# Probabilities split without GpSimd, three output tiles multiplied after the FFN loop, and DMAs issued inside attention, in a cross-attention and ternary FFN kernel

## The reference

```
x = x + xattn(layernorm(x), ctx)          # x (4, 2048, 512), ctx (4, 154, 512)
x = x + ffn(layernorm(x))
xattn: q = x @ Wq.T -> q1, q2 of 16 heads x 32;  k1, k2, v from ctx, 8 kv heads
       w = softmax(q1 k1') - lam * softmax(q2 k2');  a = w @ v
       a * rsqrt(mean(a^2) + eps) * g * (1 - lam_init) @ Wo.T
ffn:   h = gelu(layernorm(x; g1, b1) @ ternary(w1).T + bias1)      # 512 -> 2048
       layernorm(h; g2, b2) @ ternary(w2).T + bias2                # 2048 -> 512
```

## Time and profile before

| what | value |
|---|---|
| median of three runs | 2513.64 us |
| the profiled execution | 2510.21 us, span 2508.4 us |
| PE busy | 2191.9 us, 87% of the span |
| DVE, ACT, POOL busy | 76%, 58%, 54% |
| mean granted TensorE clock | 0.923 of 2.4 GHz |
| chain that ended last | PE 42%, DVE 17%, issue 9%, SPq 9%, ACT 7% |

### The profile page before, as it was taken

How to read it: one execution, slowest core, us unless ns; L and a number is a source line. 1 busy time by engine, 2 the same in 40 slices (tenths; PEclk the granted TensorE clock), 3 DMA queues, 4 the chain that set the end, 5 groups by cost and what they waited for, 6 DMA issues and landing times.

```text
span 2508.4 us, 45318 instructions
## 1 busy us (share of the span) xinstructions
PE 2191.9 (87%) x18239; PEld 1217.8 (49%) x18239; DVE 1913.5 (76%) x3030; ACT 1456.4 (58%) x1973; POOL 1344.7 (54%) x931
## 2 busy tenths in 40 slices
PE   7777979889797988989798898979889898998968
PEld 5344445445454544445454444545445454554543
DVE  4776779778687877868787786878768787877763
ACT  3574656656465665556566554656646466664544
POOL 2333737546383754638365473846537384663627
PEclk9868989999898999989899998989989898998979
DMA  8313122131312213121321313122141211312010
GB/s 292 99 45 83 28 74 63 40 81 52 85 33 73 64 40 81 50 70 36 86 65 40 81 45 73 38 70 67 40 95 40 72 44 56 81 40 64 23 30 17
DMA packets 253009, 160.16 MB, mean 64 GB/s; under 512 B 171812, under 2 KB 221580, under 8 KB 252288
## 3 DMA queue, kind: packets, MB, share of 16 engines
q1 hardware_dynamic: 249792, 152.07, 23.0%
q0 software_dynamic: 3008, 5.20, 0.7%
HBM read 51.82 MB, written 20.38 MB: 29 GB/s over the span
## 4 chain that ended last, share of the span: by engine, by line
PE 42%; DVE 17%; issue 9%; SPq 9%; ACT 7%; DMA 1%; POOL 1%; DVEq 0%; POOLq 0%; ACTq 0%
PE ps L1581 17%; PE ps L1603 9%; SPq L517 8%; PE ps L1487 5%; DVE arena L1261 3%; ACT arena L812 2%; DVE attn_raw L1146 2%; DVE attn_raw L1151 2%; PE ps L1515 2%; DVE p L1133 1%; DVE attn_raw L1155 1%; PE ps L1593 1%; ACT p L815 1%; DVE attn_raw L1160 1%; ACT arena L810 1%
## 5 line engine op out<-in xcount | busy, mean ns | idle before, releaser
L686 POOL TENSOR_TENSOR attn_raw<-attn_raw 128x512 f32<-128x512 f32 x448 | 642.4, 1453 | 51.6 <-ACT attn_raw L841 23.2
L1581 PE MATMUL ps<-rows,w1T 128*128 128x512 f16 x2048 | 491.2, 383 | 31.2 <-DVE rows L1221 31.2
L1109 DVE TENSOR_REDUCE arena<-ps 128x3 f32<-128x462 f32 (+1 forms) x704 | 403.7, 613 | 43.3 <-PE ps L1487 41.5
L1226 DVE SCALAR_TENSOR_TENSOR arena<-attn_raw,vec_cols,arena 128x512 f16<-128x512 f32 x256 | 278.6, 1088 | 62.0 <-ACT arena L839 58.5
L836 ACT ACTIVATE attn_raw<-ps,vec_cols,wstep 128x512 f32<-128x512 f32 x256 | 198.5, 775 | 183.4 <-PE ps L1581 181.4
L1581 PEld LDWEIGHTS ps<-rows,w1T 128*128 128x128 f16 x2048 | 191.9, 98 | 230.3 <-DVE rows L1221 43.5
L810 ACT ACTIVATE arena<-ps 128x1024 f32<-128x1024 f32 x128 | 130.8, 1022 | 297.5 <-PE ps L1515 297.5
L657 POOL TENSOR_TENSOR q<-q 128x512 f16<-128x512 f32 x128 | 201.8, 1578 | 169.8 <-ACT q L801 168.5
L1603 PE MATMUL ps<-w2T,arena 128*128 128x512 f16 x1088 | 271.1, 378 | 0.0
L799 ACT ACTIVATE q<-ps 128x512 f32<-128x512 f32 x128 | 77.0, 602 | 329.8 <-PE ps L1437 189.9
L664 POOL TENSOR_TENSOR p<-arena,p 128x1024 f16<-128x1024 f32 x64 | 137.8, 2153 | 242.5 <-ACT p L815 242.5
(11 more groups left out here) (195 smaller groups left out, 5073.4 us busy)
## 6 DMA issues: line engine op xcount, KB each, us to landing
stack_raw<-q SPq DMA_DIRECT2D x744, 64.0 KB, 2.0
arena<-in_x SPq DMA_DIRECT2D x64, 256.0 KB, 2.7
out<-arena SPq DMA_DIRECT2D x64, 256.0 KB, 2.0
arena<-in_x SPq DMA_DIRECT2D x14, 1024.0 KB, 5.9
arena<-in_L_ffn_w SPq DMA_DIRECT2D x7, 1024.0 KB, 14.4
rows<-in_x SPq DMA_DIRECT2D x2, 1024.0 KB, 6.9
stack_raw<-in_L_xattn_Wq SPq DMA_DIRECT2D x8, 256.0 KB, 9.2
k_att<-k_store SPq DMA_DIRECT2D x4, 495.0 KB
```

The lines of the kernel that those rows point to most:

```text
L686: ins = pool.tensor_tensor(acc[:, e, :], acc[:, e, :], src[:, j % NG, :], ALU.add)
L1109: dve.tensor_reduce(negmax[:, tt, u0:u1], ps[:, row_bank(c, tb), 0:(u1 - u0) * S].rearrange("p (u s) -> p u s", s=S), AX.X, ALU.max, negat ...
L1226: dve.scalar_tensor_tensor(gg16[:, j, 1, :], gelu_t[:, j % NG, :], g2_col[:, j:j + 1], gg16[:, j, 0, :], ALU.mult, ALU.subtract).then_inc( ...
L1581: ins = pe.matmul(ps[:, B_H + j % 2, :], w1T[:, k, j * P:(j + 1) * P], rows16[:, e, k, :], start=(k == 0 and e == 0), stop=(k == KD - 1 an ...
```

## The change

The splitting of probabilities leaves POOL: ACT casts slices 0, 1 and then 2 to 4, DVE computes lo of both parts. In the FFN loop only row tile 0 is multiplied; tiles 1, 2 and 3 are "late". The first group's upper scores go to banks 5 to 7, so that group no longer waits for the gelu sums and two output tiles; the second group does. The stores, the reloads of x, the transposes of the attention output and the first pair of query stacks are issued by SP in the order of `ATTEND`.

```diff
-    "e2 g f2 y0 y1 y2 s0 q0 z0 z1 z2 s1 h3 v0 s2 i3 v1 y3 z3 s3 q1 v2 s4 q2 t0 v3 s5 q3 v4 s6 t1 v5 s7 v6 t2 v7").split()]
+    "e1 c g e2 s0 e3 y0 y1 q0 s1 h1 v0 z0 z1 s2 h2 v1 y2 s3 q1 t0 z2 v2 s4 h3 v3 s5 h4 t1 y3 v4 s6 q2 z3 v5 s7 t2 q3 v6 v7").split()]
+LATE1 = 0
+LATE = {("e", 1): (1, LATE1, 10), ("e", 2): (1, 10, 14), ("e", 3): (1, 14, JH),
+        ("h", 1): (2, 0, 8), ("h", 2): (2, 8, JH), ("h", 3): (3, 0, 8), ("h", 4): (3, 8, JH)}
-            return 2 + tt if tt < 2 else B_Q
+            return (2, 3, B_Q, B_Q)[tt]
+        def upper_banks(c, gi):
+            return slice(2, 5) if gi or c == 0 else slice(5, 8)
...
             def iteration(i):                                # SP
-                if i:
-                    store(i - 1, 0)
-                    for tt in range(1, TT):
-                        store(i - 1, tt)
-                        load_x_res(i, tt - 1)
-                    load_x_res(i, TT - 1)
+                for what, n in ATTEND if i else ():
+                    if what == "z":
+                        store(i - 1, n)
+                        if n:
+                            load_x_res(i, n - 1)
+                    elif what == "t":
+                        transpose_attn(i, n)
+                        if n == 0 and i + 1 < NBLK:
+                            stack_queries(i + 1, 0, i)
...
-                    for p in range(0 if i else QATT // 2, QM // 2):
+                    for p in range(1 if i else QATT // 2, QM // 2):
                         stack_queries(i + 1, p, i)
...
-            def probs_lo(c, gi):                             # POOL
-                wait(pool, s_p_hi, c, 2 * QM, 2 * gi + 1)
-                split = p_split[gi % 2]
-                pool.tensor_tensor(split[:, 1, 0:2, :], probs[:, gi % 2, 0:2, :], split[:, 0, 0:2, :],
-                                   ALU.subtract).then_inc(s_lo_pool, 1)
...
-                for half in range(2):                        # ACT
+                for half, slices in enumerate((slice(0, 2), slice(2, 5))):
                     wait(act, s_p, c, 2 * QM, 2 * gi + half + 1)
-                    act.copy(split[:, 0, 2 * half:2 * half + 2, :],
-                             probs[:, buf, 2 * half:2 * half + 2, :]).then_inc(s_p_hi, 1)
+                    act.copy(split[:, 0, slices, :], probs[:, buf, slices, :]).then_inc(s_p_hi, 1)
...
-                dve.tensor_copy(split[:, 0, 4, :], probs[:, buf, 4, :]).then_inc(s_r_hi, 1)
-                wait(dve, s_p_hi, c, 2 * QM, 2 * gi + 2)
-                wait(dve, s_r_hi, c, QM, gi + 1)
-                dve.tensor_tensor(split[:, 1, 2:5, :], probs[:, buf, 2:5, :], split[:, 0, 2:5, :],
-                                  ALU.subtract).then_inc(s_lo_dve, 1)
+                for half, slices in enumerate((slice(0, 2), slice(2, 5))):
+                    wait(dve, s_p_hi, c, 2 * QM, 2 * gi + half + 1)
+                    ins = dve.tensor_tensor(split[:, 1, slices, :], probs[:, buf, slices, :], split[:, 0, slices, :],
+                                            ALU.subtract)
+                ins.then_inc(s_p_lo, 1)
...
+                elif n == 0 and c >= 2:                      # PE, queries
+                    wait(pe, s_p, c - 1, 2 * QM, 2)
                 elif n == 1:
                     if c >= 2:
-                        wait(pe, s_y, c - 2, TT, TT)
+                        wait(pe, s_y, c - 2, TT, 3)
...
+                    if n == 2 and c >= 2:
+                        wait(pe, s_y, c - 2, TT, TT)
...
                     if c:                                    # PE, scores of group 0
-                        wait(pe, s_gln, c - 1, 1, 1)
-                        wait(pe, s_y, c - 1, TT, 2)
+                        wait(pe, s_gelu, c - 1, JH, JH)
...
+                elif gi == 1 and c:
+                    wait(pe, s_p, c, 2 * QM, 1)
+                    wait(pe, s_gln, c - 1, 1, 1)
+                    wait(pe, s_y, c - 1, TT, 2)
...
                     if j == 0 and tt == 2:                   # PE, ffn_late
-                        wait(pe, s_gelu, c, JH, JH)
-                    elif j == 0:
+                        wait(pe, s_p, c + 1, 2 * QM, 2)
+                    elif j == 0 and tt == 3:
                         wait(pe, s_y, c, TT, tt)
+                        if c + 2 < NBLK:
+                            wait(pe, s_q32, c + 2, QM, 2)
+                    elif tt == 1:
+                        wait(pe, s_gg_lo, c, JH, j + 1)
...
-                banks = (2, 3) if ahead else range(TT)
+                banks = (2,) if ahead else range(TT)
```

More of the change, by code:

```diff
@@ L327, in build @@
             "row_scores", "row_max", "negmax_hi", "negmax_lo", "negmax_transposed", "negmax_copied", "negmax_stacked"))
-        s_s, s_p, s_p_hi, s_r_hi, s_lo_dve, s_lo_pool, s_pv, s_inv, s_norm, s_att = (sem(n) for n in (
-            "scores", "probs", "probs_hi", "rest_probs_hi", "probs_lo_by_dve", "probs_lo_by_pool", "values_done", "inverse_sum",
+        s_s, s_p, s_p_hi, s_p_lo, s_pv, s_inv, s_norm, s_att = (sem(n) for n in (
+            "scores", "probs", "probs_hi", "probs_lo", "values_done", "inverse_sum",
             "values_normed", "attn_ready"))
@@ L490, in load_x_in @@
                 if c >= 2:
-                    wait(sp, s_lo_dve, c - 2, QM, QM - 1)
-                    wait(sp, s_lo_pool, c - 2, QM, QM - 1)
+                    wait(sp, s_p_lo, c - 2, QM, QM - 1)
                 sp.dma_start(x_in if c >= 2 else x_in0, x_blk[c]).then_inc(s_xin, 16)
@@ L559, in iteration @@
                     transpose_ternary(JH + 12)
-                elif i + 1 < NBLK:
-                    for p in range(QATT // 2):
-                        transpose_attn(i, p)
                 if i + 1 < NBLK and (i + 1) % BLK_PER_BATCH == 0:
                     load_keys((i + 1) // BLK_PER_BATCH)
-                if i + 1 < NBLK:
+                if i:
+                    load_x_res(i, TT - 1)
+                else:
                     transpose_attn(i, KD - 2)
@@ L581, in iteration @@
                     stack_maxima(i + 1)
-                else:
-                    for mp in range(KD):
-                        transpose_attn(i, mp)
             setup()
@@ L696, in iteration @@
                         power(3, s_gln, s_rstd4, i - 1)
-                    elif what == "s":
-                        probs_lo(i, n)
                     elif what == "q" and ahead:
@@ L811, in exponentials @@
                 wait(act, s_s, c, 2 * QM, 2 * gi + 2)
-                act.activation(probs[:, buf, 2:5, :], ps[:, 2:5, :], ACT.Exp).then_inc(s_p, 1)
-                for half in range(2):
+                act.activation(probs[:, buf, 2:5, :], ps[:, upper_banks(c, gi), :], ACT.Exp).then_inc(s_p, 1)
+                for half, slices in enumerate((slice(0, 2), slice(2, 5))):
                     wait(act, s_p, c, 2 * QM, 2 * gi + half + 1)
-                    act.copy(split[:, 0, 2 * half:2 * half + 2, :],
-                             probs[:, buf, 2 * half:2 * half + 2, :]).then_inc(s_p_hi, 1)
+                    act.copy(split[:, 0, slices, :], probs[:, buf, slices, :]).then_inc(s_p_hi, 1)
             def attn_hi(c, mp):
@@ L1506, in scores @@
                     if c:
-                        wait(pe, s_gln, c - 1, 1, 1)
-                        wait(pe, s_y, c - 1, TT, 2)
+                        wait(pe, s_gelu, c - 1, JH, JH)
                     if 0 < c < NBLK - 1:
                         wait_rows(pe, s_xt_lo, s_xd, c + 1)
+                elif gi == 1 and c:
+                    wait(pe, s_p, c, 2 * QM, 1)
+                    wait(pe, s_gln, c - 1, 1, 1)
+                    wait(pe, s_y, c - 1, TT, 2)
                 else:
                     wait(pe, s_p, c, 2 * QM, 2 * gi)
+                upper = upper_banks(c, gi).start
                 for i in range(UPT):
                     u = UPT * gi + i
-                    ins = pe.matmul(ps[:, i, :], k_att[0:STKM, key_unit(u), 0:P], stack[0:STKM, u, :], start=True, stop=True)
+                    ins = pe.matmul(ps[:, i if i < 2 else upper + i - 2, :], k_att[0:STKM, key_unit(u), 0:P], stack[0:STKM, u, :], start=True, stop=True)
                     if i == 1:
@@ L1526, in values @@
                 mp, split = ORDER[gi] % (QM // 2), p_split[gi % 2]
-                wait(pe, s_lo_dve, c, QM, gi + 1)
-                wait(pe, s_lo_pool, c, QM, gi + 1)
+                wait(pe, s_p_lo, c, QM, gi + 1)
                 wait(pe, s_norm, c, QM, gi)
@@ L1629, in iteration @@
                         values(i, n)
-                    elif what == "e" and i:
-                        ffn_late(i - 1, n, range(JH // 4))
+                    elif (what, n) in LATE and i:
+                        tt, j0, j1 = LATE[what, n]
+                        ffn_late(i - 1, tt, range(j0, j1))
+                    elif what == "c" and i:
                         transpose_maxima(i)
-                    elif what == "f" and i:
-                        ffn_late(i - 1, n, range(JH // 4, JH))
```

(4 more changed lines are left out.)

6 lines of the change are left out of this document (2 added, 4 removed).

## The result

The kernel after takes **2531.78 us** (2530.05 to 2533.56), the kernel before, on the same chip, 2513.15: ratio 1.0073, 95% interval 1.006 to 1.0085, or 18.6 us slower. The forecast was 2511, with faster the likeliest side: the time lies inside the range and on the wrong side. The profiled execution has a span of 2528.2 us against 2508.4.

What follows compares the result with a forecast made beforehand. The FFN loop was held by PE, DVE and POOL together. A block's -1.3 + 4.1 - 2.6 = +0.2 gave +3 us over 14 blocks, block 0 -5, last block 0: 2511 us, range 2465 to 2550.

Steps and rivals of the forecast that it cites:

- Part 1: FFN loop: PE sheds 6.9 us but DVE doesn't follow; maxima transposed 53.15 us after loop start, against 51.83 before.
- e1, 20 matmuls, 4.3 us: Loop's end: row tile 1's 20 late matmuls behind DVE's last gelu lo, before the maxima's transposes, take 4.3 us.
- Part 2: Loop's end to first scores: scores wait for DMAs of the maxima, starting at 58.2 against 59.52, -1.3 us a block.
- Part 3: Attention: new gaps, POOL's lo of query 3 and 3.0 us of half clock give 65.2 against 61.14, +4.1 us.
- its load stays: Attention: DVE loses a cast, gains a lo of about 1.2 us, no longer meets POOL, so its load is unchanged.
- Part 4: Attention to FFN loop: early query stacks free query 6, removing 2.6 of PE's 2.63 us wait, -2.6 us a block.
- Block 0: First block's loop: PE busy 65.80 of 67.00 us, so the 6.9 us saved count, less new waits: -5 us.
- The last block: Final block of the kernel: no change, 0 us.
- Half clock and POOL stay out of attention: Faster rival: attention takes 60.8 to 62.2 us; 2469 us, or another 20 less; chance 0.26.
- The loop does shorten: Faster rival, FFN loop: gelu's lo falls towards 0.73 us, DVE ends up to 3 us earlier; 2470 us; chance 0.11.
- The opening goes to half clock: Slower rival: idle time around first scores puts 4 to 5 us at half clock; attention 68, 2550 us; chance 0.18.
- Query 6 not freed: Slower rival, before the FFN loop: SP reaches pair 1 late, the 2.6 us stay; 2548 us; chance 0.05.

Runs made afterwards that it cites:

- sp_only: Kernel before with SP's order alone changed (stores, tile reloads, attention transposes, first pair of query stacks issued inside attention): 2473.62 us, ratio 0.9851 to before.
- tiles_first: Kernel after with row tile 1 finished before the first scores and output tiles 0 and 1 added ahead of group 0's lo: 2494.98 us, ratio 0.9927 to before.
- after_tile2_first: Kernel after with one token moved, DVE adding output tile 2 ahead of group 1's normalise step: 2487.07 us, ratio 0.9886 to before.
- after_old_split: Kernel after with the old splitting of probabilities (POOL's subtractions, ACT's two casts, DVE's cast as before): 2611.13 us, ratio 1.0386 to before.
- dense_loop: Kernel after with row tile 1 multiplied twice, once more in the FFN loop, 32 unused matmuls a block: 2545.82 us, ratio 1.0128 to before.

## Why the prediction was wrong, point by point

- **Part 1, the end of the loop: right in kind, wrong in size.** That DVE doesn't follow held: in blocks 1 to 14 a lo in the loop takes 1.20 us in the mean, against 1.11 before, POOL's 28 sums still have no break, and PE idles. The last lo ends 48.94 us after the loop's start (1181.52 + 1.81 - 1134.39) where I said 48.3; beside POOL's sums it took 1.81, where it had taken 1.01. The step that failed is the next one: "e1, 20 matmuls, 4.3 us". I took full clock straight behind the idle time that I had just derived. It was 6.0, so the maxima were transposed at 55.44 and not at 53.15.
- **Part 2: its increments right, its base wrong.** From the transposes to the scores 4.85 us (forecast 4.92), released by the DMA of the maxima. Loop and tail were 60.3 us in nine of the ten blocks where the clock fell (58.2 in block 14, whose loop is shorter), and 58.6 in the four where it didn't; I said 58.2. The ten slow tails cost 10 x 1.7 = 17 us, nearly the whole 18.6 by which the kernel is slower: without them it would be within measurement of the old one. (This is the account against the forecast. By parts the same 18.6 is about -78 - 26 + 121.)
- **Part 3: total right, one claim wrong.** Attention 65.2 forecast, 64.99 measured, and the walk can be checked gap by gap: 0.95, 3.0, 2.5, 0.6 and about 4 forecast; 0.82, 2.67, 2.47, 0.50 and 4.35 in block 6. Half clock was taken at 3.0; PE is busy 54.79 us where its work at full clock is 50.6, so 4.2. POOL's lo of query 3 took 1.67 and stretched DVE's lo beside it, as I had added. But "its load stays" looked only at the steps that the diff edits, at their lengths without POOL. DVE's load fell by 4.6 us a block with the split alone, and the split is the largest gain of the change. It didn't spoil the total, because the walk used undisturbed durations for after and compared with the measured length of before. What it spoiled is the understanding: the three parts of the change are worth -78 (the split), -42 (SP's part; -26 with the split in place) and +121 (order, banks and late tiles). I took them for three small ones, and so never asked whether the order alone was bad.
- **The Trainium skill's rule** (SBUF — State Buffer, section Who interferes with whom), which I had used only for query 3's lo, bears on this same place. The trace agrees: without POOL's subtractions DVE's steps with two SBUF inputs fell from 2304 to 1758 and from 1781 to 970 ns, and the normalise step, one of whose inputs is in PSUM, stayed at 691. Had I applied it to the earlier trace rows's 25.62 us of POOL, I would have had a gain of DVE time to weigh.
- **Part 4: right.** The way to the loop 23.6 forecast (26.2 - 2.6), 23.29 measured; sp_only gives 2.1 us of it in the old order. ACT's query 6 no longer waits for a DMA.
- **The sum.** Of the 21.8 us between forecast and measured span, loop and tail account for 14.4 (14 x 1.03). Attention's +7.7 and the way to the loop's -8.0 cancel: block 6's attention of 61.14 stood for a mean of 60.34. **Block 0**, -5 forecast, came to +1.0: I counted 6.9 us of PE's work as time because PE was busy 65.80 of 67.00, yet its loop grew by 3.7 us. **The last block**, 0 forecast, came to +4.5: it has no queries but walks the same order of output tiles, and attention there grew by 3.9. Ahead of block 0 the 2.7 us are unexplained.
- **The rivals.** "Half clock and POOL stay out of attention" is out: half clock took 4.2 us there. "The loop does shorten" is out: lo did not fall. "The opening goes to half clock" came true in part. Query 0 ran at full clock (its twelve matmuls took 2.75), but behind the wait of 2.67 before the second scores the clock was half for 3.4 us in 11 of 14 blocks, a loss of 1.7 us each, where the rival had 4 to 5 us of half clock and an attention of 68. "Query 6 not freed" is out. Most of the slower side came from a place for which I had no rival: half clock behind the idle time at the loop's end. I had the row of such a gap, the 3.24 us of the earlier trace rows, and had written that PE would stand idle there, and didn't put the two together.

## What to carry to other kernels

When work is taken off an engine that isn't alone at its limit, forecast the idle time and then price what follows at the lower clock: 32 matmuls taken out of this loop were 6.9 us on paper, and putting them back gained 44 us. When an engine is relieved, look at what it had been slowing: list every operation of the other engine in that stretch against its shortest form, and not only those in the diff. Try an addition or copy that frees PE in front of whatever on its engine waits for something else; moving one token so gave 45 to 58 us here, in three kernels. Then look at what PE waits for next: a wait of 2.67 us removed before the second scores came back by 1.0 at query 0.

## What the runs showed of the hardware

- PE's granted clock fell behind a wait of 2.29 us at the end of a dense loop in 10 of 14 blocks (0.89 over the tail) and stayed at 1.00 in four, same program. Three other kernels with that loop, tiles_first, after_tile2_first and after_old_split, have it low in 12, 9 and 14 of 14. In dense_loop, with no such wait, it is 1.00 in all 14. In the kernel before, a wait of 2.63 us was followed by full clock, and one of 3.24 by half. What decides between them is open.
- A tiny DVE step on 128x4 elements took 0.17 us alone and 1.2 beside POOL's additions: so nearly all of its length was, as I read it, waiting for the other engine.
- A DVE subtraction with two inputs in SBUF (128x1536) took 1.76 us alone and up to 3.0 beside POOL's subtractions; one with an input in PSUM (128x512) took 0.69 in both cases.
- Useless PE work made a stage shorter: loop and tail took 59.2 us with 32 extra matmuls, and 60.3 without them in the blocks where the clock fell behind the wait. In the four where it stayed they took 58.6, so what the work bought was the clock. The kernel as a whole was still 14 us slower with it.
